# Retrieved experts in a two-layer transformer block on one core: row gathers replaced by dense products with one-hot matrices

## What is computed

```
xn = layernorm(x)
s  = attention of 32 heads of 8, 8 key/value groups, biases on q, k, v, out
h  = silu(xn W_up + b_up) W_down + b_down                  # 1024 wide, then 128
sim = (h W_q) . keys          # per head (8 heads) two halves of 45 scores
top 8 of each half, top 8 of the 64 sums -> index = 45 i + j, sc
z   = silu( (h . down_embed[index]) * softmax(sc) )        # 8 heads x 8 picks
out = sum of z * up_embed[index]                           # 64 rows of 256
x  = x + s * silu(out)
xn = layernorm(x)
x  = x + (attention of 16 heads of 16, 4 groups, causal, ALiBi) * silu(int8 linear(xn))
```

## Time and profile before

| quantity | value |
|---|---|
| median of 3 runs | 1010.35 us (1001.56, 1010.35, 1014.47) |
| span of the profiled execution, first to last instruction | 772.2 us |
| median less span | 238.15 us |
| mean granted TensorE clock in the span | 0.845 |
| PE, PEld busy | 581.7 us (75%), 328.9 us (43%) |
| DVE, ACT, POOL busy | 585.9 us (76%), 258.0 us (33%), 515.5 us (67%) |
| DMA | 117.38 MB, of which 100.70 MB in the gathers' queue |

### The profile page before, as it was taken

One profiled execution on the slowest core, in us unless ns is written; L12 is line 12 of the kernel. 1 busy time (PEld: TensorE's weight loads), 2 busy tenths in 40 slices (PEclk: granted clock), 3 DMA queues, 4 the chain that ended last, 5 costly groups with the idle time before them and its releaser, 6 DMA issues.

```text
span 772.2 us, 9592 instructions
## 1 busy us (share of the span) xinstructions
PE 581.7 (75%) x2418; PEld 328.9 (43%) x2435; DVE 585.9 (76%) x2701; ACT 258.0 (33%) x659; POOL 515.5 (67%) x523
## 2 busy tenths in 40 slices
PE   5612666679656757999956669999855789999997
PEld 4401354223543335454335436445332354445572
DVE  2687987979859998749789998867599985567550
ACT  3300132444431113545314223545311144353222
POOL 5277777777777777777777777777777777760000
PEclk9855778799887767999977878999976799999778
DMA  8167555555775555555765555557755565550000
GB/s 286 42 183 220 154 168 156 156 160 153 198 222 165 159 154 157 155 155 166 204 203 153 145 154 155 147 152 202 215 167 157 154 170 155 156 151 1 14 1 14
DMA packets 43882, 117.38 MB, mean 152 GB/s; under 512 B 10479, under 2 KB 17775, under 8 KB 43410
## 3 DMA queue, kind: packets, MB, share of 16 engines
q0 software_dynamic: 32768, 100.70, 46.2%
q1 hardware_dynamic: 10662, 15.88, 7.0%
q10 hardware_dynamic: 396, 0.20, 0.1%
HBM read 113.52 MB, written 3.01 MB: 151 GB/s over the span
## 4 chain that ended last, share of the span: by engine, by line
PE 36%; POOL 28%; DVE 16%; issue 11%; DMA 7%; ACT 1%; SPq 1%; ACTq 0%; POOLq 0%; DVEq 0%
POOL rows L561 28%; PE turn L726 7%; PE outs L794 6%; PE experts L860 4%; DVE nmax L1258 4%; PE scores L775 3%; DVE hot L1225 3%; PE scores L763 3%; DVE acc L1250 3%; DMA rows<-experts_table,idx 3%; DMA stackk<-scratchk 2%; PE turn L684 2%; DMA stackq<-nmaxT 1%; PE outs L805 1%; PE turn L596 1%
## 5 line engine op out<-in xcount | busy, mean ns | idle before, releaser
L561 POOL DMA_INDIRECT rows<-experts_table,idx x512 | 504.8, 986 | 171.6 <-issue 153.5
L1225 DVE CUSTOM_DVE_ANT_0 hot<-rows,h 128x128 f32<-128x128 f32 x512 | 114.4, 285 | 47.0 <-DMA rows<-experts_table,idx 46.8
L860 PE MATMUL experts<-rows,diag 128*128 128x256 f32 x384 | 131.1, 492 | 23.2 <-ACT diag L1074 22.6
L1031 ACT ACTIVATE probs<-scores 128x512 f32<-128x512 f32 x176 | 99.0, 595 | 126.9 <-PE scores L775 50.7
L710 PE MATMUL turn<-stackk,stackq 125*128 125x256 bf16 x256 | 58.2, 341 | 91.7 <-DVE nmax L1258 51.8
L1250 DVE SCALAR_TENSOR_TENSOR acc<-rows,zs,acc 128x256 f32<-128x256 f32 x304 | 125.5, 476 | 0.6
L860 PEld LDWEIGHTS experts<-rows,diag 128*128 128x128 f32 x384 | 89.4, 245 | 57.5 <-ACT diag L1074 27.6
L1258 DVE TENSOR_REDUCE nmax<-turn 128x2 f32<-128x512 f32 x128 | 82.4, 680 | 5.2 <-PE turn L710 5.1
L1074 ACT ACTIVATE diag<-ident,zs 128x128 f32<-128x128 f32 x192 | 62.9, 392 | 45.6 <-DVE zs L1235 45.6
L1068 ACT ACTIVATE zt<-za 128x8 f32<-128x8 f32 x64 | 13.3, 208 | 192.1 <-DVE za L1229 192.1
L710 PEld LDWEIGHTS turn<-stackk,stackq 125*128 125x128 bf16 x256 | 21.5, 111 | 130.2 <-DVE nmax L1258 79.3
(11 more groups left out here) (157 smaller groups left out, 717.3 us busy)
## 6 DMA issues: line engine op xcount, KB each, us to landing
rows<-experts_table,idx POOLq DMA_INDIRECT x512, 3.1
stackq<-scratchq SPq DMA_DIRECT2D x12, 384.0 KB
scratchq<-parts SPq DMA_DIRECT2D x4, 384.0 KB, 3.2
stackk<-scratchk SPq DMA_DIRECT2D x12, 96.0 KB
xnext<-x SPq DMA_DIRECT2D x4, 256.0 KB, 3.7
wup<-w_wup SPq DMA_DIRECT2D x1, 1024.0 KB, 5.1
xres<-x SPq DMA_DIRECT2D x4, 256.0 KB, 3.5
y<-gate SPq DMA_DIRECT2D x3, 256.0 KB, 2.2
```

What stands on the lines that cost most here:

```text
L561: nc.gpsimd.indirect_dma_start(rows[:, slot, c, :], None, tab, bass.IndirectOffsetOnAxis(ap=idx[:, b % 2, t, TOP * h + c:TOP * h + c + 1], ...
L860: ins = mm(experts[:, s // FH, :], diag[:, g % 2, k, :], rows[:, g % RING, k, PRIV:ROW], start=(s % FH == 0 and k == 0), stop=(s % FH == F ...
L1031: fn(probs[:, at % PROBS, :], scores[:, at % SCORES, :], ACT.Exp).then_inc(exp_done[layer], 1)
L1225: ins = v.tensor_tensor_reduce(out=zjunk[:, k, :], in0=rows[:, slot, k, 0:PRIV], in1=h2[:, b % 2, t, :], scale=1.0, scalar=0.0, op0=ALU.mu ...
```

## The change

The gathers, and all that worked on gathered rows, are removed: the indirect DMAs, the ring, `dots`, `tanh` and `diag` by group, `add`, the accumulations on DVE, `keep`. Also gone is the early pick of the first heads. In their place, for every batch:

1. **table** (PE, new L708; 8 pieces of 2 float32 matmuls of 128x128 weights by 256 columns): the dot products of h with all 2048 down rows. An expert's place in the table is written as a high digit of 128 values and a low digit of 16, so a bank holds two low digits of 128 high ones for 256 tokens.
2. **firsts** (ACT copy to bf16), **left** (DVE L1302, subtract), **seconds** (POOL L612 and L614: copy to bf16, subtract): three bf16 parts `dots` of those numbers, 8 pieces of 512 columns per step.
3. **places** (DVE): splits each picked index in its two digits. The high ones are stored in DRAM and read back by SP, repeated over all 128 partitions, as `same`: 4 quarters of 1 MB per batch, into two buffers that lie in the tile `shared`. **match** (DVE L1311, 4 per batch, 128x4096 in bf16) compares each with the partition's number in place, which gives one-hot matrices. **turnw** (PE, 3 transposes) with copies on ACT gives digits and weights pick-major; **low one-hot** (DVE L1318, 128x4096) the low digits' one-hot.
4. **pick** (PE L721; 8 pieces of 48 matmuls): for each of 128 positions t (the pair of tokens t of both tiles, whose 64 + 64 picks fill 128 columns) the one-hot matrix of the picks, as weights, times its 32 columns of `dots`, in three parts. DVE multiplies with the low one-hot and sums (L1327, L1329: 512 columns, 8 times), multiplies by the weights (L1333), ACT takes tanh twice, DVE makes the factors and their three bf16 parts (L1338 to L1342).
5. **onehot** (POOL L625, 128 instructions of 128x128 per batch) makes the one-hot matrices the other way round, **scale** (DVE L1349, 8 of 128x1536 in bf16) the low one-hots times the factors' parts, **spread** (PE L732; 8 pieces of 48 matmuls of 32 columns) multiplies the two, which gives for each token its weight on each of the 2048 experts. ACT copies it out (8 of 512 columns) into the space of `dots`, so the next batch's `firsts` wait for the `mix`.
6. **mix** (PE L742; 2 tiles of 16 float32 matmuls of 256 columns): the weights times all 2048 up rows. SP loads `up_table` (2 MB) once per batch, after the batch's last pick, over the space of `same`. ACT copies the result (`mixed`).

PSUM is one pool of 6 banks (`BANKS`), and each PE plan word names its bank or banks after a slash; the scores use the same pool. The room for dynamic DMA descriptors is set to 1024 (16384 is the default). All four plans are written anew, and POOL has one (`POOL_PLAN`). In the built programs PE's matmuls go from 1548 to 4624, 3072 of which are the 32-column ones; POOL's DMAs from 512 to none, its computing instructions from none to 576; DVE's 1024 custom instructions (512 with 512 reads) to none; ACT's activations from 658 to 485.

```diff
@@ -52,16 +52,19 @@
-ROW = PRIV + D
-FIRST_HEADS = 2
-GROUPS = TT * FH
-ON_PE = 3
-RING, PROBS, SCORES, TURNS = 4, 4, 3, 3
-FACTORS = 4
+PICKS = FH * TOP
+PROBS, BANKS = 4, 6
+LO, HI = 16, 128
+SPAN = TT * LO
+CHUNK = 16
+CHUNKS = P // CHUNK
+QUARTERS = 4
...
 PE_PLAN = """
-    norm0:0.0 up:0.0 up:0.1 up:0.2 up:0.3 fold:0.0 down:0.0 sim:0.0 qkv0:0.0 keep:0.0 sim:0.1 add:0.0 max0:0.0 max0:0.1 add:0.1
...
+    norm0:0.0/0 up:0.0/1 up:0.1/2 up:0.2/3 fold:0.0/45 up:0.3/0 down:0.0/1 sim:0.0/23 table:0.0/4 sim:0.1/50 table:0.1/1
...
@@ gpsimd
-            for g in range(B * GROUPS):
...
-                if g >= RING:
-                    pool.wait_ge(up_done, g - RING + 1)
-                    pool.wait_ge(acc_done, g - RING + 1)
-                for c in range(TOP):
-                    nc.gpsimd.indirect_dma_start(
...
+            def seconds(b, n):
+                use = LOADS * b + n
+                pool.wait_ge(drained["table"], use + 1)
+                at = dots[:, :, 1, :, PER_BANK * n:PER_BANK * (n + 1)]
+                nc.gpsimd.tensor_copy(at, left[:, use % RESTS, :, :, :]).then_inc(seconds_ready, 1)
+                pool.wait_ge(seconds_ready, use + 1)
+                nc.gpsimd.tensor_tensor(dots[:, :, 2, :, PER_BANK * n:PER_BANK * (n + 1)], left[:, use % RESTS, :, :, :], at,
+                                        ALU.subtract).then_inc(thirds_ready, 1)
+            def one_hot(b, n):
...
+                pool.wait_ge(drained["turnw"], b + 1)
+                wait_from(pool, filled["spread"], use - ONE_HOTS + 1)
+                for k in range(CHUNK):
+                    t = CHUNK * n + k
+                    nc.gpsimd.tensor_scalar(high_hot[:, use % ONE_HOTS, k, :], iotah[:, :], turnedh[:, t:t + 1], None, ALU.is_equal)                        .then_inc(high_hot_ready, 1)
@@ sync
+            def load_up_table(b, _):
+                sp.wait_ge(filled["pick"], CHUNKS * (b + 1))
+                sp.dma_start(full(up_table), w["up_table"]).then_inc(up_table_in, 16)
@@ tensor
-            def add(_, g):
...
-                pe.wait_ge(diag_ready, g + 1)
-                for k in range(ON_PE):
-                    ins = mm(experts[:, s // FH, :], diag[:, g % 2, k, :], rows[:, g % RING, k, PRIV:ROW],
...
+            def table(b, n):
...
+                for k in range(PER_BANK):
+                    ins = mm(ps[:, k * S:(k + 1) * S], down_table[:, PER_BANK * n + k, :], h2T[:, :], start=True, stop=True)
+            def pick(b, n):
+                if n == 0:
+                    pe.wait_ge(firsts_ready, LOADS * (b + 1))
+                    pe.wait_ge(thirds_ready, LOADS * (b + 1))
+                q = n // (CHUNKS // QUARTERS)
+                pe.wait_ge(same_ready, QUARTERS * b + q + 1)
...
+                        ins = mm(ps[:, k * SPAN:(k + 1) * SPAN], same[:, (QUARTERS * b + q) % 2, t % QUARTER, :],
+                                 dots[:, t, a, :, :].rearrange("p u l -> p (u l)"), start=(a == 0), stop=(a == PARTS - 1))
+            def spread(b, n):
+                use = CHUNKS * b + n
+                pe.wait_ge(high_hot_ready, CHUNK * (use + 1))
+                pe.wait_ge(scaled_ready, use + 1)
...
+                        ins = mm(ps[:, k * SPAN:(k + 1) * SPAN], high_hot[:, use % ONE_HOTS, k, :], scaled[:, use % SCALED, k, a, :],
+            def mix(b, t):
+                if t == 0:
+                    pe.wait_ge(drained["spread"], CHUNKS * (b + 1))
+                    pe.wait_ge(up_table_in, 16 * (b + 1))
...
+                for k in range(LO):
+                    ins = mm(experts[:, t, :], spreads[:, k, t, :], up_table[:, k, :], start=(k == 0), stop=(k == LO - 1))
@@ vector
-                for k in range(TOP):
-                    ins = v.tensor_tensor_reduce(
-                        out=zjunk[:, k, :], in0=rows[:, slot, k, 0:PRIV], in1=h2[:, b % 2, t, :],
...
-                        ins = v.scalar_tensor_tensor(total, row, factor, total, ALU.mult, ALU.add)
...
+            def match(b, q):
...
+                v.tensor_scalar(at, at, own[:, 0:1], None, ALU.is_equal).then_inc(same_ready, 1)
+            def pick(b, n):
...
+                v.tensor_tensor(full(picks), ps[:, :].rearrange("p (t l) -> p t l", l=SPAN), low_hot[:, at, :], ALU.mult).then_inc(drained["pick"], 1)
+                dve.wait_ge(drained["pick"], use + 1)
+                c.link(v.tensor_reduce(z[:, at], full(picks), AX.X, ALU.add))
+            def scale(b, n):
...
+                v.tensor_tensor(scaled[:, use % SCALED, :, :, :], low_hot[:, at, :].unsqueeze(2).broadcast_to(shape),
+                                factors[:, at, :].unsqueeze(3).broadcast_to(shape), ALU.mult).then_inc(scaled_ready, 1)
```

More of the change, by code:

```diff
@@ L79 @@
[L79 to L82, removed]
@@ new lines @@
+    spread:0.0/4 max0:0.22/0 spread:0.1/5 max0:0.23/4 max0:0.24/2 max0:0.25/5 max0:0.26/3 spread:0.2/0 max0:0.27/1 max0:0.28/4
+    max0:0.29/2 spread:0.3/0 down:1.0/0 max0:0.30/0 spread:0.4/5 spread:0.5/3 max0:0.31/5 sim:1.0/13 spread:0.6/4 sim:1.1/13
+    spread:0.7/2 mix:0.0 nm0:0.0/4 mix:0.1 sc0:0.0/0 table:1.0/1 sc0:0.1/3 table:1.1/2 sc0:0.2/5 pv0:0.0 sc0:0.3/4 sc0:0.4/0
+    sc0:0.5/3 pv0:0.1 sc0:0.6/5 pv0:0.2 sc0:0.7/4 table:1.2/1 sc0:0.8/0 pv0:0.3 sc0:0.9/3 sc0:0.10/5 sc0:0.11/4 pv0:0.4
@@ L197 @@
 """
 SP_PLAN = """
-    x:0.0 weights:0.0 weights:0.1 weights:0.2 weights:0.3 x:1.0 ones:0.0 res:0.0 store0:0.0 stack0:0.0 x:2.0 x:3.0 store0:1.0
-    stack0:1.0 res:1.0 store0:2.0 stack0:2.0 res:2.0 out:0.0 store0:3.0 stack0:3.0 res:3.0 out:1.0 out:2.0 out:3.0 out:3.1
-"""
-PER_BATCH = {"norm0": 1, "up": CB // 2, "down": 1, "fold": 2, "sim": 2 * TT, "keep": 1, "qkv0": 2, "max0": H0, "nm0": 1,
+    x:0.0 weights:0.0 res:0.0 x:1.0 weights:0.1 weights:0.2 weights:0.3 x:2.0 ones:0.0 weights:0.4 store0:0.0 stack0:0.0
@@ new lines @@
+    high:0.0 same:0.0 same:0.1 same:0.2 same:0.3 table:0.0 x:3.0 high:1.0 same:1.0 same:1.1 store0:1.0 stack0:1.0 res:1.0
+    same:1.2 same:1.3 table:1.0 high:2.0 same:2.0 same:2.1 store0:2.0 stack0:2.0 res:2.0 same:2.2 same:2.3 table:2.0 out:0.0
+    high:3.0 same:3.0 same:3.1 store0:3.0 stack0:3.0 res:3.0 same:3.2 same:3.3 table:3.0 out:1.0 out:2.0 out:3.0 out:3.1
+"""
+PER_BATCH = {"norm0": 1, "up": CB // 2, "down": 1, "fold": 2, "sim": 2 * TT, "turnw": 1, "table": LOADS,
+             "pick": CHUNKS, "spread": CHUNKS, "mix": TT, "qkv0": 2, "sc0": UNITS[0], "sc1": UNITS[1], "max0": H0, "nm0": 1,
@@ L1168, in top_lookup @@
                 c.settle()
-                c.link(v.tensor_copy(bestf[:, :, hd, :], bestij[:, :, hd, :]))
-                whole = end - first == FH
-                views = [(slice(0, 2 * FH), full(bestf).rearrange("p a h k -> p (a h) k"), full(topf).rearrange("p a h k -> p (a h) k"),
-                          full(picked).rearrange("p a n -> p (a n)"))] if whole else \
-                    [(slice(FH * a + first, FH * a + end), bestf[:, a, hd, :], topf[:, a, hd, :], picked[:, a, TOP * first:TOP * end])
-                     for a in range(2)]
```

674 lines of the change are left out of this document (371 added, 303 removed).

## The result

The changed kernel takes 870.26 us, the median of 4 runs (864.95 to 872.88); the kernel before 1006.51 us in the same comparison. The ratio is 0.862, with a 95% interval of 0.856 to 0.868. The forecast was 1015 us, no change, with 815 to 1110 as its range: the time lies in the range, but the change is a gain of 14%, which the likeliest case did not have.

A forecast was written before the change was run, and what follows sets the result against it. PE was taken to bound: 743 us of work less 25 for the clock, 718/0.93 = 772, plus 20 for batch 0, less 15 of stack wait, span 777; plus 238 outside it, 1015 us. Range 815 to 1110.

The forecast's parts named there:

- the likeliest case: F, chance 0.42: PE bounds and the 238 us stay, 975 to 1075 us, forecast 1015.
- The 238 us: Kernel before: 1010.35 us less the traced span of 772.2, taken as time in which no recorded instruction runs.
- F: Whole kernel: PE bounds at 62 ns per short matmul, the 238 us stay; 975 to 1075 us; chance 0.42.
- G: Time outside the span goes with the gathers, falling to 15 to 50 us; 779 to 900 us; chance 0.30.
- The gathers as the pace: Kernel before, POOL: gathers of 1.25 us each, 640 us for 512, 28% of the chain, pace the whole.
- Short matmuls: PE, pick and spread: 3072 matmuls at 62 ns, 191 us; bounds 135 and 301 us.
- The clock: PE: fuller, so nearer 0.95 than 0.845; the old 450 us of work gets 25 us shorter.
- POOL's one-hots: POOL, before spread: 0.25 us each, 32 us per batch, no cost; bounds 0.12 and 0.95 us each.
- DVE: VectorE: 265 us out, 232 in, total 515 to 553 us, less than PE, so no cost in the mean.
- The wait for the stacks' trip: Stacks' trip through DRAM: of 29.6 us of waiting, half goes, 15 us, as table and pick stand before it.
- Batch 0: Start of the kernel: one batch's chain runs alone; 20 us kept beyond the 7% of waits.
- The span: First to last recorded instruction: 772 + 20 - 15 = 777 us, as it was.

The follow-up runs named there:

- the second trace: The kernel before, run unchanged for another profile: time 1028.09 us, span 1026.3 us.

## Why the prediction was wrong

- **The 238 us: the step that failed.** The prediction took them as time outside the span and gave F's assumption, that they stay (0.42), more weight than G's (0.30), although its own chances for "faster" summed to 0.55. G's outcome came true, that they go with the gathers, and its 779 to 900 us hold the measured time; but that is in part luck, since its picture, like F's, was wrong: they are not around the kernel but inside its usual execution, as waits of the other engines while gathers are issued. A median 31% above the traced span meant that the trace was of another kind of execution, and the pace and chain read from it weren't those that the median measures: the second trace has a span of 1026.3 us, with 1.8 us outside. F's argument that "the traced pace of the gathers is steady" was read from the wrong execution. The Trainium skill, "Runtime: NRT & Kernel Launch", "The ~15µs preamble/postamble breakdown", gave some 15 us; every run here with both on record shows 1.8 us between span and time, which is less and is what counts here. Either way a rest of 238 us can't be start and end, and the prediction had this argument and gave it too little weight.
- **The gathers as the pace.** In the first trace POOL had 28% of the chain; in the second 1%. With fewer of them the unknown waits of DVE, PE and ACT shrink, and this is where their removal gains. How a gather does it isn't shown. Shown is that it goes with the number of gathers, not with their bytes or packets, for the most part not with the custom instruction, and that it is less with a small room for descriptors, where they follow one another more slowly. Why one execution with all 512 was free of it stays open.
- **Short matmuls: mis-sized.** 62 ns taken, 44 as the lower bound, 27 measured: 3072 x 27 = 83 us, not 191. L616 is float32, and I had scaled by columns and not by type; a float32 matmul leaves two such records. The 98 ns of a weight load are the length of a record, and these overlap. The Trainium skill ("TensorE: Matmul & The Clock Gate", "Back-to-back issue gap") gives 81 ns per pair at 128 columns; this stream of 32 columns took a third of that, so the figure doesn't carry over to it.
- **The clock: wrong sign.** The old work was to become 25 us shorter at a warmer clock. The clock fell from 0.845 to 0.800, and the old groups grew (L836, which is L726 before, from 56.5 to 71.4 us). Where PE waited for POOL's one-hots, from 300 to 340 us, it was granted 0.50. Against the executions that are timed it is the other way round: there the kernel before had 0.725 to 0.751, and 69.1 us for L726. PE's total: 743 - 25 = 718 forecast; 743 - 108 = 635 with the short ones as measured, and 661 measured, so the clock and the rest took 26 us more.
- **POOL's one-hots: the step that the span failed on.** "I take 0.25 us and no cost." They took 0.72 us, within the bounds of 0.12 and 0.95. "No cost" was wrong: 92 us per batch (128 x 0.72) fit in a batch of 190 us only if they may be made at any time. They stand between the picks and the spread of one batch, with two buffers, so POOL first waits for PE's spread (105.8 us), then PE for POOL (123.6 us). In the rivals I even wrote that POOL can't pace the kernel, from the total of 486 us. Moving half of them to DVE took 77 us off the span (863.1 to 786.2), so the cost left out was at least about that.
- **DVE**: 515 us against 515 to 553. Right in the total, but not in its parts: the matches took 21 us in place of 79 (1.3 us for 4096 bf16 columns), scale 57 as against 59, and with these the sum would be 493, so some 22 us of smaller work were left out.
- **The wait for the stacks' trip**: from 29.6 to 17.2 us, 12 of the 15 forecast.
- **Batch 0**: 20 us kept. The stretch from 60 to 170 us alone has 60 us of idle PE, and 34 of them end with a one-hot of POOL.
- **The span**: 777 + (661 - 718) for PE's work, + 143 for idle time (202 us measured, 59 in the sum) = 863. Of the 202 us, 124 end with a one-hot of POOL.

## What to carry to other kernels

Compare the median of the runs with the span of the trace before anything else: when they differ by much more than a few us, the trace is not of the execution that is timed, and the chain in it explains something else; the first experiment is then a second trace. Time on a helper engine hides only between the moment when its input is known and the moment when its output is asked for, with the buffers in between: compare its work with that stretch, not with the span. A matmul's price is the distance between starts in a row of the same type.

## What was not expected of the hardware

- 3072 bf16 matmuls of 128x128 weights by 32 columns, each with its own weight load, start every 25 to 27 ns: 27 at a granted clock of 0.50, 25 at 1.00.
- The gathers' disturbance: with 512 gathers DVE had 234 us of waits that nothing recorded explains, with 384 92 us, with 256 20 us, and the same 231 us with 512 gathers of mostly a third of the bytes.
- POOL's one-hots take 596 ns at the median and up to 5774. POOL's timeline while DVE runs match and scale, and just after (28 of them at 0.71 us):

```profile
94.78 6.87 POOL L625 TENSOR_SCALAR high_hot<-iotah,turnedh 128x128 bf16<-128x128 bf16 x5
105.67 19.90 POOL L625 TENSOR_SCALAR high_hot<-iotah,turnedh 128x128 bf16<-128x128 bf16 x28 [4.01 <-PE turn L732]
```

DVE in the same time:

```profile
95.97 1.27 DVE L1311 TENSOR_SCALAR shared<-shared,own 128x4096 bf16<-128x4096 bf16 x1
97.16 1.84 DVE L1349 TENSOR_TENSOR scaled<-low_hot,factors 128x1536 bf16<-128x1536 bf16 x1
...
99.53 1.74 DVE L1349 TENSOR_TENSOR scaled<-low_hot,factors 128x1536 bf16<-128x1536 bf16 x1
```

Five one-hots take 6.87 us there, 1.37 each. Of the 512, 48 are longer than 0.9 us and hold 102 of the 379 us, and what overlaps them is mostly DVE's bf16 instructions (45 us of L1349, 17 of L1318, 13 of L1311), beside 16 us of the float32 maximum L1371, which overlaps the short ones for 46 us as well. That the bf16 ones hold POOL up is read from the overlap alone; no run took it apart.
